# State-space scan with an FP4 feed-forward layer: GpSimd takes the product with C a set at a time by turns, odd units ring over eight states, and dt times x moves to GpSimd

## The reference, cut to what matters

```python
u = silu(xp[:, :-2] * conv_w[0] + xp[:, 1:-1] * conv_w[1] + xp[:, 2:] * conv_w[2])
B, C = split(u @ W_bc + b_bc)                       # 16 + 16 per row
dt = softplus((u @ W_dt + b_dt) @ W_dtp + b_dtp)    # 128 per row
# for each feature d and state n, along the rows l:
#   h[l] = exp(A[d, n] * dt[l, d]) * h[l-1] + B[l, n] * (dt[l, d] * x[l, d])
#   y[l, d] = sum over n of C[l, n] * h[l]
x1 = layernorm(x + y + x * Dcoeff)
h = silu(q4(x1) @ q4(w_gate).T) * (q4(x1) @ q4(w_up).T)
out = layernorm(x1 + q4(h) @ q4(w_down).T)
```

## Time and profile before

| | us |
|---|---|
| median of three timed runs | 333.2 (332.24 to 334.01) |
| the profiled execution | 332.06 |
| its span, first to last instruction | 330.0 |
| VectorE busy | 303.8 |
| GpSimd busy | 265.6 |
| PE busy | 256.4 |
| ScalarE busy | 248.4 |

### The profile page before, as it was taken

One profiled execution on the slowest core, in us unless ns is written; L12 is line 12 of the kernel. 1 busy time (PEld: TensorE's weight loads), 2 busy tenths in 40 slices (PEclk: granted clock), 3 DMA queues, 4 the chain that ended last, 5 costly groups with the idle time before them and its releaser, 6 DMA issues.

```text
span 330.0 us, 4001 instructions
## 1 busy us (share of the span) xinstructions
PE 256.4 (78%) x1158; PEld 127.1 (39%) x1158; DVE 303.8 (92%) x336; ACT 248.4 (75%) x534; POOL 265.6 (80%) x140
## 2 busy tenths in 40 slices
PE   2576877668964997979798978879693969788994
PEld 1122322114411434634354425434351436336684
DVE  3869998999999999999999999999999699998973
ACT  2468879757876688898878997888888486656574
POOL 0076676589539999899999999999999998997771
PEclk9959999989996998999989999999999599999999
DMA  3690572910093006420470219010921000100003
GB/s 44 151 212 19 127 163 45 204 37 0 2 198 89 2 1 151 105 57 7 97 160 1 64 33 204 19 32 3 207 48 33 2 0 0 32 3 0 0 7 91
DMA packets 19261, 21.85 MB, mean 66 GB/s; under 512 B 6112, under 2 KB 15144, under 8 KB 19240
## 3 DMA queue, kind: packets, MB, share of 16 engines
q1 hardware_dynamic: 18520, 21.05, 28.1%
q10 hardware_dynamic: 720, 0.56, 0.9%
HBM read 2.72 MB, written 2.10 MB: 15 GB/s over the span
## 4 chain that ended last, share of the span: by engine, by line
POOL 40%; DVE 22%; issue 15%; PE 9%; ACT 8%; SPq 3%; ACTq 1%; DMA 1%; DVEq 0%; POOLq 0%
POOL product L898 19%; DVE db L1150 8%; DVE states L1170 7%; POOL qh_norm L938 5%; POOL qh_magic L918 3%; POOL qh_norm L913 3%; POOL hq L948 3%; SPq L510 3%; ACT ps_decay L566 2%; DVE dt_rep L1170 2%; PE ps_f L1571 2%; POOL qx_norm L924 2%; ACT L556 2%; POOL qx_magic L918 1%; POOL qx_norm L913 1%
## 5 line engine op out<-in xcount | busy, mean ns | idle before, releaser
L898 POOL TENSOR_TENSOR product<-states,c_rep 128x1024 f32<-128x1024 f32 x59 | 139.5, 2382 | 23.6 <-DVE states L1170 20.8
L566 ACT ACTIVATE ps_decay<-dt_rep,aneg 128x512 f32<-128x512 f32 x128 | 87.1, 691 | 23.9 <-DVE states L1170 17.7
L1170 DVE TENSOR_TENSOR_SCAN states<-ps_decay,db 128x512 f32<-128x512 f32 x64 | 74.9, 1202 | 0.3
L1150 DVE SCALAR_TENSOR_TENSOR db<-ps_b,bbc_rep,dt_rep 128x2048 f32<-128x2048 f32 x31 | 72.1, 2325 | 0.6 <-PE ps_b L1523 0.6
L1170 DVE TENSOR_TENSOR_SCAN states<-ps_decay,states,db 128x512 f32<-128x512 f32 x54 | 66.6, 1260 | 1.0 <-ACT ps_decay L566 1.0
L1517 PE MATMUL ps_prep<-u_feat,wbc_rep 128*128 128x512 f32 x56 | 34.0, 692 | 11.9 <-ACT c_rep L643 10.7
L1523 PE MATMUL ps_b<-u_feat,wbc_rep 128*128 128x512 f32 x64 | 36.6, 655 | 5.1 <-DVE db L1150 5.1
L556 ACT ACT_TABLE_LOAD x26 | 33.4, 1283 | 0.5
L1481 PE MATMUL ps_y<-product,gather 128*32 128x512 f32 x248 | 32.7, 614 | 1.0 <-POOL product L898 1.0
L643 ACT ACTIVATE c_rep<-ps_prep,bbc_rep 128x512 f32<-128x512 f32 x28 | 19.1, 682 | 8.5 <-PE ps_prep L1517 8.5
L1565 PE MATMUL ps_f<-gate_t,xq_t 128*128 128x352 f32 x48 | 18.7, 514 | 7.8 <-ACT hidden L650 6.5
(11 more groups left out here) (257 smaller groups left out, 495.7 us busy)
## 6 DMA issues: line engine op xcount, KB each, us to landing
dt_rep<-dtx SPq DMA_DIRECT2D x124, 128.0 KB, 2.4
x_tok<-in_L_attn_x SPq DMA_DIRECT2D x8, 256.0 KB, 3.0
out<-y_out SPq DMA_DIRECT2D x7, 256.0 KB, 2.3
dt_rep<-dtx ACTq DMA_DIRECT2D x4, 128.0 KB, 3.7
out<-y_out SPq DMA_DIRECT2D x2, 128.0 KB, 1.8
hidden<-in_L_ffn_w_down SPq DMA_DIRECT2D x1, 176.0 KB, 3.4
x_feat<-in_L_attn_x SPq DMA_DIRECT2D x8, 0.5 KB, 2.1
hidden<-in_L_ffn_w_gate SPq DMA_DIRECT2D x1, 128.0 KB, 2.8
```

Source lines behind the costliest of these rows:

```text
L566: nc.scalar.activation(ps_decay[BANK_OF[i]][:], dt_rep[p][:, c, 0, :], ACT.Exp, scale=aneg[:, c, m:m + 1]).then_inc(decay_done, 1)
L898: nc.gpsimd.tensor_tensor(product[:, j % PRODUCTS], groups(s, 2 * j, 2), over(c_rep[p][:, j // SET_PAIRS, :], 2), ALU.mult).then_inc(produ ...
L1150: nc.vector.scalar_tensor_tensor(out=db[m % DB][:], in0=over(ps_b[:], QUADS), scalar=bbc_rep[:, 0, m:m + 1], in1=dt_rep[p][:, :, 1, :], op ...
L1170: nc.vector.tensor_tensor_scan(out=groups(s, k, 1)[:, 0, :], data0=ps_decay[BANK_OF[s.at(GROUPS, k)]][:], data1=db[k // QUADS % DB][:, k % ...
```

## The change

The product with C is made for a set's four groups in one operation of 2048 elements. Its three operands are seen through `in_turn`, which walks two neighbouring elements of group 0, the same two of groups 1, 2 and 3, and then goes on to the next two; C's pair is the same for all four. The counters of products go from pairs to sets. `states[1]` gets eight places, an odd unit's scan k waits from k = 8 on for the set that held its place, and the last unit no longer uses `c_rep[0]`. dt times x is made by GpSimd from the SBUF copy of dt, at the same places of the step, and the second softplus on ScalarE is gone; TensorE's first matmul for C waits for dt alone.

```diff
-PRODUCTS = 2 * SET_PAIRS
-ODD_STATES = 6
+PRODUCTS = 2
+ODD_STATES = 8
...
+def in_turn(t):
+
+    return t.rearrange("p g (t b) -> p t g b", b=2)
...
-        product = sb("product", [128, PRODUCTS, 2, UNIT])
+        product = sb("product", [128, PRODUCTS, QUADS, UNIT])
...
-        last_states = [states[1][:], dt_rep[0][:].rearrange("p c i t -> p (c i) t"), c_rep[0][:]]
+        last_states = [states[1][:], dt_rep[0][:].rearrange("p c i t -> p (c i) t")]
...
                 nc.scalar.activation(dtx[:, 0, :], ps_prep[:], ACT.Softplus, bias=bz[:]).then_inc(dt_out, 1)
-                nc.scalar.activation(ps_prep[:], ps_prep[:], ACT.Softplus, bias=bz[:]).then_inc(dt_done, 1)
...
-            def times_c(s, j, p):
-                pool.wait_ge(scan_done, s.at(GROUPS, 2 * j + 2))
...
-                nc.gpsimd.tensor_tensor(product[:, j % PRODUCTS], groups(s, 2 * j, 2),
-                                        over(c_rep[p][:, j // SET_PAIRS, :], 2), ALU.mult).then_inc(product_done, 1)
+            def times_c(s, m, p):
+                pool.wait_ge(scan_done, s.at(GROUPS, QUADS * (m + 1)))
...
+                    pool.wait_ge(sum_done, s.at(SETS, m - PRODUCTS + 1))
+                nc.gpsimd.tensor_tensor(in_turn(product[:, m % PRODUCTS]), in_turn(groups(s, QUADS * m, QUADS)),
+                                        in_turn(over(c_rep[p][:, m, :], QUADS)), ALU.mult).then_inc(product_done, 1)
+
+            def dtx_of(a, o):
+                pool.wait_ge(dt_out, a.at(1, 1))
+                for c in range(QUADS):
+                    pool.wait_ge(dt_in[c], a.at(16 * STATES))
+                nc.gpsimd.tensor_tensor(dtx[:, 1, :], dtx[:, 0, :], x_feat[o][:, 1:UNIT + 1], ALU.mult).then_inc(dtx_done, 1)
...
-                    if s is not None and k % 2 and (a is not None or k < GROUPS - QUADS):
-                        times_c(s, k // 2, p)
+                    if a is not None and k == prep_places(a)["pool dtx"]:
+                        dtx_of(a, 1 - p)
+                    if k % QUADS == QUADS - 1 and (a is not None or k < GROUPS - QUADS):
+                        times_c(s, k // QUADS, p)
...
-                elif p == 1 and k >= ring:
-                    dve.wait_ge(product_done, s.at(PAIRS, (k - ring) // 2 + 1))
-                elif s.beyond(2):
-                    dve.wait_ge(product_done, s.at(PAIRS, (k - ring - GROUPS) // 2 + 1))
+                if p == 1 and k >= ring and s.first < UNITS - 1:
+                    dve.wait_ge(product_done, s.at(SETS, (k - ring) // QUADS + 1))
+                elif s.beyond(2) and (s.first < UNITS - 1 or k < ring):
+                    dve.wait_ge(product_done, s.at(SETS, (k - ring - GROUPS) // QUADS + 1))
...
-            def dtx_of(a, o):
-                dve.wait_ge(dt_done, a.at(1))
-                for c in range(QUADS):
-                    dve.wait_ge(dt_in[c], a.at(16 * STATES))
-                nc.vector.tensor_tensor(dtx[:, 1, :], ps_prep[:], x_feat[o][:, 1:UNIT + 1],
-                                        ALU.mult).then_inc(dtx_done, 1)
...
-                    pe.wait_ge(dtx_done, a.at(1, 1))
+                    pe.wait_ge(dt_out, a.at(1, 1))
```

More of the change, by code:

```diff
@@ L87 @@
     "act C": (4, 7, 9, 10), "act r": 0, "act r variance": 3, "act x1": 3, "act xq": 12, "act hq": 3,
-    "act variance": 10, "act y": 11, "act x square": 7, "act h square": 7, "dve db": (15, 3, 7, 11), "dve dtx": 1,
+    "act variance": 10, "act y": 11, "act x square": 7, "act h square": 7, "dve db": (15, 3, 7, 11), "pool dtx": 1,
     "dve tiles": (GROUPS, GROUPS, GROUPS + 1, GROUPS + 1),
@@ L97 @@
     "pe x": 0, "pe conv": (1, 2), "pe z": 3, "pe C": (7, 9, 10, 11), "act x": 0, "act window": 4,
-    "act C": (7, 8, 9, 11), "dve dtx": 6,
+    "act C": (7, 8, 9, 11), "pool dtx": 6,
 }
@@ L887, in _ @@
             order_x, order_h = Order(pool, x_code_order, POOL_CODES), Order(pool, h_code_order, POOL_CODES)
[L889 to L899 removed]
+            def times_c(s, m, p):
+                pool.wait_ge(scan_done, s.at(GROUPS, QUADS * (m + 1)))
+                if not s.beyond(1):
+                    pool.wait_ge(head_c_done, m + 1)
+                elif m == 0:
+                    pool.wait_ge(prep_evac, s.at(PREP_EVAC, PREP_EVAC))
+                if s.beyond(1) or m >= PRODUCTS:
+                    pool.wait_ge(sum_done, s.at(SETS, m - PRODUCTS + 1))
[6 more added lines that the diff above has]
+                nc.gpsimd.tensor_tensor(dtx[:, 1, :], dtx[:, 0, :], x_feat[o][:, 1:UNIT + 1], ALU.mult).then_inc(dtx_done, 1)
             def norm_of(f):
@@ L1231, in times_last_c @@
             def times_last_c(s, k):
-                j = k // 2
+                m, c = k // QUADS, k % QUADS
                 dve.wait_ge(scan_done, s.at(GROUPS, k + 1))
                 dve.wait_ge(prep_evac, s.at(PREP_EVAC, PREP_EVAC))
-                dve.wait_ge(sum_done, s.at(SETS, (j - PRODUCTS) // SET_PAIRS + 1))
+                dve.wait_ge(sum_done, s.at(SETS, m - PRODUCTS + 1))
                 nc.vector.scalar_tensor_tensor(
-                    out=product[:, j % PRODUCTS, k % 2, :], in0=ps_prep[:], scalar=bbc_rep[:, 1, SETS - 1:SETS],
+                    out=product[:, m % PRODUCTS, c, :], in0=ps_prep[:], scalar=bbc_rep[:, 1, SETS - 1:SETS],
                     in1=groups(s, k, 1)[:, 0, :],
@@ L1264, in step @@
                             gate(f, k, early)
-                    if a is not None and k == prep_places(a)["dve dtx"]:
-                        dtx_of(a, 1 - p)
             def tail(f, g, h, p):
@@ L1474, in sum_states @@
                     pe.wait_ge(head_c_done, SETS)
[L1475 removed]
+                pe.wait_ge(product_done, s.at(SETS, m + 1))
                 if m == 0:
@@ L1481, in sum_states @@
                     last = nc.tensor.matmul(ps_y[c * E:(c + 1) * E, :], gather[:],
-                                            product[:, (m * SET_PAIRS + c // 2) % PRODUCTS, c % 2, :],
+                                            product[:, m % PRODUCTS, c, :],
                                             start=False, stop=(m == SETS - 1))
```

9 lines of the change are left out of this document (1 added, 8 removed).

## The result

| | before | after |
|---|---|---|
| median, us | 333.33 (332.24 to 334.01) | 343.17 (342.02 to 344.72) |
| profiled execution, us | 332.06 | 342.02 |
| its span, us | 330.0 | 340.2 |

The kernel after is slower: the ratio of the times is 1.0301, 95% interval 1.0242 to 1.0361. The forecast was 329.0 us, with a range of 326.5 to 334.0.

The account below looks back on a forecast made before the run. VectorE was taken to set the pace at 35.03 us a step, GpSimd close behind. Savings of 6 x 0.60 + 0.65 = 4.25 us from 333.2 gave 328.95, say 329.0 us; range 326.5 to 334.0 us.

Parts of the forecast that it names:

- Part 2: GpSimd's product with C: a set's operation of 2048 elements takes 3.85 us, ends 3.69 and 4.53.
- Part 1: dt times x leaves VectorE: 6 x 0.60 us, plus 0.65 for the second softplus in unit 1's step, 4.25 us.
- The model by fresh input bytes: GpSimd's cost per element rises by 0.11 ns per fresh input byte; with C kept, 1.79 ns an element.
- Part 3: dt times x arrives on GpSimd: 1.27 us, low end 1.06; hidden under VectorE's 34.43 us step up to T = 4.4.
- The wait ahead of the copies: SyncE's replications queue behind dt times x on GpSimd; last issued 3.6 us later, 10 us remain, costed at nothing.
- Part 4: Coarser hand-over, a set waits for its fourth scan: norm of x not delayed, 0.3 us of cover.
- the ring: Eight places for odd units' states: over 8 us of VectorE work before scan 8, so it costs nothing.
- the last sum: On TensorE, gets set 3 at T after the last scan, where a 2.36 us pair stood; hardly later.
- the first: Rival: C not kept, product 4.53 us, GpSimd's step 34.9 us; kernel 331.0 us, or 332; chance 0.16.
- The jump: Rival: 2 KB between pairs of states costs extra fetches, T 5.4 or 6.3 us; kernel 345 to 362 us; chance 0.12.
- The term for the clock: TensorE's lower granted clock near 256 us: one such stretch more or less is worth up to 2 us, no sign.
- The third rival: A moved wait, in GpSimd's queue or ScalarE's chain, idles VectorE and eats the gain: 331.5 to 334 us; chance 0.08.

Follow-up runs that it names:

- the cut step: Kernel after, with VectorE's bf16 step for the h codes cut into 16 and 1392 columns: 344.03 us (one run).
- the plain order: Kernel after, with each set's product as one operation over 2048 contiguous elements, no turns: 356.31 us (one run).
- the halves: Kernel after, with each set's product by turns cut into two operations of 256 columns: 332.96 us, ratio 1.0004 to the kernel before.
- the fastest kernel: Kernel after, x codes at place 7, GpSimd's x operations at 6, TensorE's second B matmul at 0, second sum at 12: 329.23 us, ratio 0.9899.

## Why the prediction was wrong

**The step that failed** is one that the sum doesn't have: what a longer operation of GpSimd costs the VectorE instruction that can't run beside it. Part 2 met the trace of it, the pair of 2646 ns among pairs of 2358, called it interference, and left in 0.2 us a step for GpSimd. It is the hold seen from GpSimd's side. I didn't ask which VectorE instruction ran beside that pair (it starts at 209.30; the h step runs from 208.96 to 209.73), nor why a step of 1408 columns took 836 ns where one of 1120 took 452 in the same trace. With that, the step would have been costed so: set 1's product starts when scan 7 ends, the h step stands behind scan 8 and so about 1 us into the product; it ends 0.38 us after it, at 3.85 - 1.0 + 0.38 = 3.2 us, 2.4 more than now, six times on the engine that sets the pace: 14.4 us, and 343 us in all. Measured were 2.44 us, six times, 14.6 us. Shown by the cut step, the plain order and the halves.

**Part 1, right.** 0.61 us a step was measured. In unit 1's step the second softplus was to give 0.65. There VectorE waits for the decay in both kernels (0.98 and 1.01 us), so the gain is what ScalarE lost ahead of it: from its first table load to that decay it takes 5.20 us now (48.71 to 53.91) and took 5.75 (49.31 to 55.06), 0.55 us.

**Part 2, right in its number, wrong in its reason.** 3.876 us for 3.85. The model by fresh input bytes doesn't hold: in plain order two fresh fp32 operands cost (3811 - 182)/2048 = 1.77 ns an element where they lie at different offsets from a multiple of 64 bytes, and 2.12 where they lie at the same. The row of two fresh operands that I drew it from was of the second kind. So the floor of 2.1 ns that the prediction took from the Trainium skill (GPSIMD Engine Reference; its 2.5 cycles stand in section 2.1, Instruction dispatch, and not in section 3) and saw borne out by that row is no floor here.

**Part 3.** 1.09 us, between the ends given. The wait ahead of the copies cost nothing in the steps after the first, and nothing in the kernel after as a whole, but with pairs it costs 3.65 us once, over the halo load and a convolution at the lower clock: the set product is what makes room in the first step.

**Part 4** looked for delays behind the longer operation: the norm of x, the ring, the last sum. The ring of eight and the norms cost nothing, as said. The last sum was called hardly later; it made VectorE wait 2.5 us in unit 1's step, because TensorE had the next spreading of B queued behind it. In the later steps the same wait doesn't appear.

**The rivals.** The price of the first, 4.53 us for C not kept, didn't come. That C is kept isn't shown by this: in plain order, which walks C anew for each group, 3.81 us are enough once C lies elsewhere. The jump, my slower case, has the right sign by luck and the wrong mechanism: the steps of 2 KB cost nothing, (3876 - 182)/2048 = 1.80 ns an element. The rule of the Trainium skill that the prediction weighed there (GPSIMD Engine Reference, section 7, Performance pitfalls for Q7 kernels: 2.9 instead of 1.9 cycles for a step over 8 bytes) would have made it an estimated 6.8 us; the trace, with 3.88, doesn't show it for pairs of neighbours. The term for the clock: VectorE's longest wait for the up product fell from 2.06 to 0.45 us, inside the 2 us kept for it. The third rival, a moved wait, came as 1.9 us for `ps_b` and not for `dt_rep` or a decay, where I looked for it; with dt times x moved alone it ate the whole gain.

**The forecast itself** is met once the h step is kept away from the product: 329.23 us, and a step of 34.41 us for 34.43. That it fits so closely is in part luck: that kernel has moves on TensorE that the forecast didn't know, and its h step is 0.2 us shorter than in the kernel before.

## What to carry to other kernels

Before one instruction of an engine is made longer, list what the neighbouring engine can't run beside it: an instruction whose duration in the trace depends on when it starts, and whose end follows another engine's end by a constant, is held, and its cost is set by the length of the operation it meets and not by its own. Such a hold counts as busy time, so compare the mean of each form with its like before reading waits. And where two engines take turns on one thing, put the sensitive instruction among the other's short operations before merging the long ones.

## What the runs showed of the hardware

VectorE's contiguous bf16 step (the h step) is shut out while a GpSimd operation that started before it runs, at 16 columns as at 1408, and ends 0.03 us after it with 16 columns and 0.38 us with 1408. In the kernel before, the x step (528 columns, read from padded blocks) took 0.40 us in the middle of a pair, and the fp32 scans are not held either; why these are exempt stays open. The kernel before, VectorE and then two pairs of GpSimd in one row:

```profile
105.47 0.40 DVE L1110 TENSOR_SCALAR qx_magic<-x_square 128x528 bf16<-128x528 bf16 x1
...
101.68 4.94 POOL L898 TENSOR_TENSOR product<-states,c_rep 128x1024 f32<-128x1024 f32 x2
```

GpSimd's products of two fp32 operands in plain order take 20% more for each element where the two lie a multiple of 64 bytes apart (2.12 ns) than at the other distances that these kernels have, 24 to 60 bytes more than that (1.77 ns); by turns a multiple of 2048 costs 1.80 ns. C shifted by one element in plain order, together with the moves of the fastest kernel, wasn't tried.
